# Second attention of a two-layer transformer kernel: a new order of four things inside its tile loop

## The reference

```
h = layernorm(x, ln1_g, ln1_b) + shift                # shift from the condition
q, k, v = (h @ Wqkv.T) split in 16 heads of 64
q = layernorm(q, qn_g, qn_b);  k = layernorm(k, kn_g, kn_b)   # over the 64 of a head
p = softmax(q @ k.T / 8)
o = p @ v
x = x + o @ Wout.T
gate logits = x @ Wgate.T                              # routing of the experts, later
```

## Time and profile before

| | |
|---|---|
| median of three runs | 2740.92 us (2740.9 to 2741.17) |
| the profiled execution's own time | 2738.47 us |
| its span, first to last instruction | 2736.6 us |
| mean granted TensorE clock | 0.962 of full speed |
| busy: PE, DVE, ACT, POOL | 90%, 72%, 56%, 38% of the span |
| second attention | about 965 to 2215 us |

### The profile page before, as it was taken

The page is one execution under the profiler, slowest core; times in us unless marked ns, Lnnn a source line. Parts: engine busy times, 40 slices in busy tenths (PEclk is TensorE's granted clock), DMA queues, the critical chain, the costliest instruction groups (busy, mean ns, idle before and its releaser), DMA issues. The chain is left out here.

```text
span 2736.6 us, 68347 instructions
## 1 busy us (share of the span) xinstructions
PE 2449.6 (90%) x25691; PEld 2091.2 (76%) x25692; DVE 1970.6 (72%) x3788; ACT 1521.0 (56%) x2847; POOL 1044.3 (38%) x876
## 2 busy tenths in 40 slices
PE   5999999969999979999999999999999933799997
PEld 4777777759999957777777777777777723799996
DVE  4888888746666667777877777777777758666663
ACT  3777777646666545555555555555555512565653
POOL 2677676620000023433334333343433401355543
PEclk9999999979999989999999999999999966899999
DMA  4111111001110100000000000000000020234332
GB/s 117 32 32 34 35 31 35 26 20 30 29 29 29 27 35 17 12 15 12 15 15 12 15 12 15 15 12 15 12 15 13 14 58 16 88 78 107 78 71 31
DMA packets 86351, 89.19 MB, mean 33 GB/s; under 512 B 26752, under 2 KB 80640, under 8 KB 83584
## 3 DMA queue, kind: packets, MB, share of 16 engines
q1 hardware_dynamic: 73984, 71.08, 8.5%
q0 software_dynamic: 12288, 17.05, 3.8%
HBM read 62.40 MB, written 25.69 MB: 32 GB/s over the span
## 5 line engine op out<-in xcount | busy, mean ns | idle before, releaser
L963 POOL TENSOR_TENSOR a_rq<-a_vq,minus_half 128x8 f32<-128x8 f32 x256 | 423.7, 1673 | 165.3 <-DVE a_vq L978 165.3
L913 ACT ACTIVATE a_sq<-a_bqk 128x512 f32<-128x512 f32 x256 | 152.2, 595 | 346.0 <-PE a_bqk L117 345.7
L958 POOL TENSOR_TENSOR a_rstd<-a_veps,minus_half 128x1 f32<-128x1 f32 x64 | 35.3, 552 | 651.2 <-DVE a_veps L1022 651.2
L115 PE MATMUL a_bqk<-wqk_hi,a_h_lo 128*128 128x512 f32 x512 | 206.4, 403 | 36.4 <-DVE a_h_lo L1001 36.4
L1054 DVE TENSOR_TENSOR a_qk<-a_bqk,a_rq 128x512 f32<-128x512 f32 x256 | 170.6, 687 | 80.1 <-POOL a_rq L963 80.0
L116 PE MATMUL a_bqk<-wqk_lo,a_h_hi 128*128 128x512 f32 x512 | 201.2, 393 | 0.0
L117 PE MATMUL a_bqk<-wqk_hi,a_h_hi 128*128 128x512 f32 x512 | 201.1, 393 | 0.0
L1154 PE MATMUL a_bqk<-consts_sb,a_qk 128*128 128x128 f32 x1024 | 140.9, 280 | 57.3 <-DVE a_qk L1054 57.3
L1641 DVE TENSOR_TENSOR e_u_lo<-e_u,e_u_hi 128x512 fp32r<-128x512 f32 x128 | 88.9, 694 | 127.2 <-ACT e_u_hi L1504 123.8
L431 POOL TENSOR_TENSOR a_kbd<-a_kT,consts_sb 128x512 f32<-128x512 f32 x128 | 130.9, 1044 | 123.2 <-PE a_bs L556 120.2
L1499 ACT ACTIVATE e_u<-e_bu,e_b 128x512 f32<-128x512 f32 x128 | 88.3, 690 | 156.6 <-PE e_bu L117 150.8
(11 more groups left out here) (243 smaller groups left out, 8024.7 us busy)
## 6 DMA issues: line engine op xcount, KB each, us to landing
X<-in_x SPq DMA_DIRECT2D x64, 128.0 KB
a_gate<-gates_of_rows SPq DMA_DIRECT2D x128, 64.0 KB, 2.5
m_gate<-gates_of_rows SPq DMA_DIRECT2D x32, 256.0 KB, 4.4
tokens<-a_xs SPq DMA_DIRECT2D x64, 128.0 KB, 1.7
out<-a_xs SPq DMA_DIRECT2D x64, 128.0 KB, 1.7
e_w<-in_fc1s SPq DMA_DIRECT2D x8, 1024.0 KB, 4.8
e_w<-in_fc2s SPq DMA_DIRECT2D x8, 1024.0 KB, 6.9
a_w<-in_fc_w SPq DMA_DIRECT2D x2, 1024.0 KB, 6.3
```

The lines of the kernel that those rows point to most:

```text
L115: tensor.matmul(to, w_lo, x_hi, start=start, stop=False)
L913: nc.scalar.activation(sq[:, n * BK:(n + 1) * BK], b_qk[:, n * BK:(n + 1) * BK], ACT.Square).then_inc(s["sq"], 1)
L963: nc.gpsimd.tensor_tensor(rq[:, 8 * n:8 * n + 8], vq[:, 8 * n:8 * n + 8], g.mhalf[:, 0:8], ALU.pow).then_inc(s["rq"], 1)
```

## The change

Four edits, all in `attention1_phase`:

1. On DVE, the sums and moments of the squares of groups 1, 2 and 3 no longer stand in one row behind the softmax: group 1's stand between the row sums and the reciprocal, groups 2's and 3's behind the probabilities, with the multiplication of group 0 between them.
2. On PE, the two transposes that turn `xhat` of the next tile stand in the middle of the output product, behind the wait for the second half of o_lo, and not after it.
3. On DVE, hT, h_hi and h_lo of the next tile stand ahead of the residual sum, and not behind it.
4. On ACT, the copies of v are split: the two pieces of the first half stand behind the squares, ahead of the copies of gate logits and transposed probabilities; the two of the second half stay where all four were. Each of the four raises the semaphore `v_out`, and PE waits for 4 per tile.

```diff
 ACT
+                    def values_out(n):
+                        act.wait_ge(s["v"], 2 * i + n + 1)
+                        for b in range(2):
+                            nc.scalar.copy(vs[n * S:(n + 1) * S, turn % 2, b, :],
+                                           b_a[b * S:(b + 1) * S, n * BK:(n + 1) * BK]).then_inc(s["v_out"], 1)
...
+                    if has(0):
+                        values_out(0)
                     if has(-2):
                         act.wait_ge(s["lg"], i - 1)
                         nc.scalar.copy(g.lg[:, :, bass.ds(i - 2, 1)], b_b[1][:, 0:E].unsqueeze(2))\
...
                     if has(0):
-                        for n in range(2):
-                            act.wait_ge(s["v"], 2 * i + n + 1)
-                            for b in range(2):
-                                last = nc.scalar.copy(vs[n * S:(n + 1) * S, turn % 2, b, :],
-                                                      b_a[b * S:(b + 1) * S, n * BK:(n + 1) * BK])
-                        last.then_inc(s["v_out"], 1)
+                        values_out(1)
 DVE
+                    def scaled(n):
+                        if n == 0 and later(i):
+                            dve.wait_ge(s["qkT"], i)
+                        dve.wait_ge(s["rq"], QG * i + n + 1)
+                        nc.vector.tensor_tensor(
...
-                    if has(-2):
-                        dve.wait_ge(s["proj"], i - 1)
...
                     if has(0):
                         dve.wait_ge(s["xT"], i + 1)
...
                         nc.vector.tensor_tensor(h_lo[:, :, :], hT[:, :, :], h_hi[:, :, :].bitcast(F32), ALU.subtract)\
                             .then_inc(s["h_lo"], 1)
+                    if has(-2):
+                        dve.wait_ge(s["proj"], i - 1)
...
                         nc.vector.reduce_sum(sm[:, :], pr[:, :, :], AX).then_inc(s["summed"], 1)
+                    if has(0):
+                        sums(1)
+                        moments(1)
+                    if has(-1):
                         dve.wait_ge(s["summed"], i)
                         nc.vector.reciprocal(rs[:, :], sm[:, :]).then_inc(s["recip"], 1)
...
                     if has(0):
-                        for n in range(1, QG):
-                            sums(n)
-                            moments(n)
+                        sums(2)
+                        moments(2)
+                        scaled(0)
+                        sums(3)
+                        moments(3)
...
                     if has(0):
-                        for n in range(QG):
...
+                        for n in range(1, QG):
+                            scaled(n)
 PE
-                        pe.wait_ge(s["v_out"], i)
+                        pe.wait_ge(s["v_out"], 4 * i)
...
+                    def turn_next():
+                        pe.wait_ge(s["xhat"], i + 2)
+                        for c in range(DC):
+                            last = nc.tensor.transpose(b_b[1][:, c * P:(c + 1) * P],
+                                                       xhat[:, c * P:(c + 1) * P], ident)
+                        last.then_inc(s["xT"], 1)
...
                             if kc % (H // 4) == 0:
                                 pe.wait_ge(s["o_lo"], 2 * (i - 1) + kc // (H // 4) + 1)
+                                if kc and has(1):
+                                    turn_next()
...
                         last.then_inc(s["proj"], 1)
-                    if has(1):
-                        pe.wait_ge(s["xhat"], i + 2)
...
+                    elif has(1):
+                        turn_next()
```

More of the change, by code:

```diff
@@ L974, in sums @@
                             .then_inc(s["red"], 1)
+                    def scaled(n):
[3 more added lines that the diff above has]
+                        nc.vector.tensor_tensor(
+                            qk[:, n * BK:(n + 1) * BK].rearrange("p (h d) -> p h d", d=HD1),
+                            b_qk[:, n * BK:(n + 1) * BK].rearrange("p (h d) -> p h d", d=HD1),
+                            rq[:, 8 * n:8 * n + 8].unsqueeze(2).to_broadcast([P, 8, HD1]), ALU.mult)\
+                            .then_inc(s["qkn"], 1)
                     def moments(n):
@@ L1002, in step @@
                             .then_inc(s["h_lo"], 1)
+                    if has(-2):
+                        dve.wait_ge(s["proj"], i - 1)
+                        if later(i - 2):
+                            dve.wait_ge(s["stored"], 32 * (i - 2))
+                            dve.wait_ge(s["xsT"], i - 2)
+                        nc.vector.tensor_tensor(xs[:, :], g.X[:, i - 2, :], b_b[0][:, 0:D], ALU.add)\
+                            .then_inc(s["res"], 1)
                     if has(0) and not later(i):
```

## The result

The changed kernel takes 2660.35 us, median of four runs (2659.45 to 2662.52), against 2740.91 us before: ratio 0.9707, 95% interval 0.969 to 0.9724. The profiled execution spans 2657.6 us, 79.0 less than before.

A forecast was written before the change was run, and what follows sets the result against it. PE was taken to set the pace: 19.05 - 1.92 of losses + 0.89 stall + 0.10 turning = 18.12 us per tile, 0.93 less over 62 tiles, 58 us, giving 2683 us; range 2666 to 2708.

The forecast's parts named there:

- The three losses of 1.06, 0.14 and 0.72 go: PE's lost time per tile before the last four qk transposes, output product and next qk product goes: 1.92 us together.
- A new stall of 0.89 at the logits copy: PE's second four probability transposes wait for ACT's logits copy, behind two v copies: 0.89 us per tile, bounds 0.75 to 1.0.
- The qk transposes: On PE, each taken at 0.114 us, from eight probability transposes in 0.91; twelve need 1.37, the last four 0.46.
- Turning from transposes back to products costs one longer step: I charge 0.10: On PE in the middle of the output product: one longer step, 0.10 us per tile, between 0 and 0.2.
- The end of the tile: On PE, the two residual transposes before the next qk product need 0.23 us.
- Probs 0.84 later, hidden by the stall: On DVE, group 1's sums and moments delay probs by 0.84 us, costing PE 0.2 unless hidden by the stall; slack 0.6.
- The residual is not late: On DVE behind h, the residual is done at 1.0 to 1.2 us, due at 1.2: no wait, bound 0.2.
- Rival 2, probs held by the pow: On DVE, probs start at 7.3 instead of 5.75 behind POOL's pow: period 18.57, 2711 us; chance 6%.
- Rival 1, the V copies don't hold PE: Logits copy on ACT is in time after all: 17.23 us per tile, 2628 us; chance 5%.
- Rivals 3, 4 and 5: Residual late behind h, 2708 us, 7%; clock falls to 1.2 GHz, 2786 us, 3%; no effect, 2741 us, 3%.

The follow-up runs named there:

- e8_one_piece_first: Changed kernel with ACT's order: logits copy, one piece of v's first half, transposed probabilities, other piece, second half of v; ratio 0.9541, 2615 us.
- e1_v_together: Changed kernel with all four copies of v again behind the copies of the transposed probabilities on ACT; ratio 0.9584, 2627 us.
- e5_turn_behind: Changed kernel with the next tile's transposes back behind the output product on PE, h still ahead of the residual; ratio 0.9902, 2714 us.
- e7_only_v_halves: Kernel before with only the copies of v split, the first half ahead of the logits copy; ratio 0.9998, 2740 us.
- e3_sums_in_a_row: Changed kernel with sums and moments of groups 1 to 3 again in one row behind the probabilities on DVE; ratio 0.9772, 2679 us.

## Why the prediction was wrong, step by step

The step that failed is the sum of a tile, in the sizes of its terms and not in their kind: the new stall (0.89 us, measured 0.81), the sixteen qk transposes in one piece (1.83, measured 1.73) and the charge for turning back to products (0.10, measured 0). The transposes' pace had no bound of its own in the range.

- **The three losses of 1.06, 0.14 and 0.72 go**: right, all three. Neither wait is in the trace after, and with ACT's order mended as well (e8_one_piece_first) a tile takes 17.0 us, close to the 19.05 - 1.92 = 17.13 that the sum by starts had. The profile's own idle times, 1.41, would have given too little; the starts were the right measure. One reason was incomplete: I had the 0.14 at the output product go with the multiplications, and wrote of the copies of v that PE gains nothing where they are taken away, since o_hi had come in time. With edits 1 to 3 alone (e1_v_together) a wait of 0.2 for o_lo is there, and it is ACT's row of four copies that makes it. Edit 4 takes it away (e8_one_piece_first has neither this wait nor the stall), so the number came out only because edits 1 and 4 were made together.
- **A new stall of 0.89 at the logits copy**: right in place, cause and kind, and measured 0.81, inside its bounds. ACT started its copies 0.03 after values(0) ended and not 0.12. PE resumed at 8.56 after the tile's first matmul, forecast 8.60, and values(1) came at 8.97, forecast 9.05.
- **The qk transposes**: here the sum failed by 0.10. I took 0.114 for each of sixteen, from eight in 0.91. The last of them, on PE's timeline:

```profile
1507.31 0.27 PE L1173 MATMUL a_bqk<-consts_sb,a_qk 128*128 128x128 f32 x1
```

  The product follows at 1507.34, only 0.03 after that start. All sixteen take 1.73 (from 1505.61), not 1.83. The eight in 0.91 held three slower steps, the first and the two at the change to the second four (0.14, 0.14 and 0.16 where the others took 0.11), which I had spread over all.
- **"Turning from transposes back to products costs one longer step: I charge 0.10"**: wrong, 0. The output product with the two transposes inside takes 3.14 from its first matmul to the scores (1507.34 to 1510.48), the same as before with the transposes behind it (1524.91 to 1528.05 in the earlier trace rows). The longer first matmul after a transpose is there (0.20, 1508.93 to 1509.13), but the transposes had a price in their old place too: two of them and the step to the scores took 0.31 (1527.74 to 1528.05), while in the middle they take 0.13 (1508.80 to 1508.93) and the last matmul is followed by the scores after 0.20. I had charged the new change of kind and not credited the old one.
- The end of the tile (residual's transposes to qk, 0.19 where I had 0.23 and a rounding) makes the rest. Together the tile took 17.79 where 18.12 stood: 0.08 up to values(1), 0.10 transposes, 0.10 turning, 0.05 others, times 61 is 20 us of the 22.6 that the forecast missed. 1 us more lies outside the 61 tiles, and 1.6 in the step from the profiled execution to the median: I carried over the 2.45 of before, and it is 0.9 here.
- **The range**: each of these was small, and all went the same way. The upper gain that I allowed, 1.17, had the stall at 0.75 and turning at 0, and kept no room for the pace of the transposes and the end of the tile, for which I gave no bounds at all. With 0.10 for the one and 0.05 for the other the bound is 1.32; 1.26 came.
- **Probs 0.84 later, hidden by the stall**: hidden, yes; 0.66 later, shown above.
- **The residual is not late**: right, 0.3 of slack; e5_turn_behind shows where it is late.
- **Rival 2, probs held by the pow**: did not come. The pow of group 1 starts at 1499.70, probs start 0.11 later and take their normal 1.22, as in all 64 tiles (1.224 to 1.226 us). The rule of the Trainium skill that was weighed there (page "SBUF — State Buffer", section "SBUF: two separate sides": the shared port pair is locked for a whole instruction) would have held probs for 1.5 us; the trace after does not agree for a pow on eight values per partition, as the earlier trace rows had suggested.
- **Rival 1, the V copies don't hold PE**: not in this kernel, but e7_only_v_halves shows that it is true in the kernel before, since its slack hides them. I had priced edit 4 rightly only because the chain behind it was removed by edit 1 at the same time. **Rivals 3, 4 and 5** did not come; the clock stayed at 1.00.

What was not tried: whether the 17.0 us of e8_one_piece_first can be lowered. There PE has no gap by the modelled ends, so fewer or cheaper matmuls are what is left to try, and no experiment touched them.

## What to carry to other kernels

Sum a change of order along the one engine that sets the pace, by start-to-start times, and price each moved group at the pace of the same group in the trace; where a move puts a change between kinds in a new place, look what the change cost in the old one. Give every term of the sum a bound, the small ones too: the range failed by terms that had none. The price of an edit depends on which others stand beside it: the same halves of v cost nothing before and 34 us after, the same spread sums are worth 72 us alone and 18 us with the stall (64 and 22 by the traces' 61 tiles), and two edits that look separate can be worth something only together; so test each alone and each left out. And in an engine's fixed row, put the short copy that another engine waits for ahead of the long ones that nobody waits for yet: that was worth 27 us for the logits copy alone, and 46 with only one piece of v ahead of the copies of the transposed probabilities.

## What the runs showed of the hardware

- Transposes of 128 by 128 on PE that follow each other start 0.11 us apart at a granted clock of 1.00 (sixteen and the step to the product in 1.73), and two of them within a row of fp32r products of 128x256 cost no more than two at its end.
- On DVE an independent instruction starts 0.08 before the end of the one ahead (1498.74 against 1497.60 + 1.22 = 1498.82), while a dependent one starts 0.04 after it (1516.16 against 1516.12); the same pair of values stands in each of some 20 tiles of either trace. So the pair of sums and moments, 0.68 and 0.17 long, added only 0.66 where it was put between two dependent instructions.
- The output product's twelve matmuls of a half took 1.46 us in some tiles and kernels (1507.34 to 1508.80 above) and up to 1.53 in others at the same granted clock (from 1519.67 to 1521.20 in e3_sums_in_a_row). In the kernel before both appear in neighbouring tiles. What makes the difference was not found.
